# The carry of a chunked scan added by identity matmuls, a contraction over pairs of time steps, and stores issued from ScalarE

## The reference

```
deltaBC = layernorm(x) @ W_bc.T          # gives dt_r (64), B (32), C (32) of each time step
delta   = softplus(dt_r @ W_dt.T + b_dt)                    # (b, l, d)
for t in time:
    h = exp(delta_t * A) * h + (delta_t * u_t) * B_t        # (b, d, n), fp32
    y_t = sum over n of h * C_t                             # (b, d)
x = x + y + u * D_param                                     # then the second layer
```

## Time and profile before

| | us |
|---|---|
| median of 3 runs | 1120.57 |
| the profiled execution | 1123.69 |
| its span, first to last instruction | 1122.0 |
| VectorE busy | 964.6 (86%) |
| TensorE busy (matmuls) | 911.9 (81%) |
| TensorE weight loads | 562.7 (50%) |
| ScalarE busy | 460.1 (41%) |
| GpSimd busy | 392.1 (35%) |

### The profile page before, as it was taken

One profiled execution on the slowest core, in us unless ns is written; L12 is line 12 of the kernel. 1 busy time (PEld: TensorE's weight loads), 2 busy tenths in 40 slices (PEclk: granted clock), 3 DMA queues, 4 the chain that ended last, 5 costly groups with the idle time before them and its releaser, 6 DMA issues. The chain is left out here.

```text
span 1122.0 us, 22454 instructions
## 1 busy us (share of the span) xinstructions
PE 911.9 (81%) x7152; PEld 562.7 (50%) x7152; DVE 964.6 (86%) x1164; ACT 460.1 (41%) x887; POOL 392.1 (35%) x690
## 2 busy tenths in 40 slices
PE   5654673489999999999999999999997856666662
PEld 4343442356656656556566566565553444343442
DVE  6664664099999999999999999999998599999993
ACT  2545544434444444444444444444431333333320
POOL 6435432233333333333333333333343244444321
PEclk9675555589999999999999999999998977787786
DMA  9399995931211112121111211111142001111001
GB/s 319 64 147 205 162 135 131 134 108 50 64 52 59 54 52 64 51 62 53 59 55 50 66 51 61 55 55 57 52 139 70 16 0 57 56 56 56 19 19 37
DMA packets 206068, 85.68 MB, mean 76 GB/s; under 512 B 139220, under 2 KB 196052, under 8 KB 205268
## 3 DMA queue, kind: packets, MB, share of 16 engines
q1 hardware_dynamic: 206036, 85.30, 31.9%
HBM read 45.85 MB, written 39.42 MB: 76 GB/s over the span
## 5 line engine op out<-in xcount | busy, mean ns | idle before, releaser
L1439 DVE TENSOR_TENSOR_SCAN arena<-arena,psum 128x1024 f32<-128x1024 f32 x256 | 585.4, 2287 | 8.9
L1260 ACT ACTIVATE arena<-psum 128x512 f32<-128x512 f32 x512 | 281.9, 605 | 347.5 <-PE psum L1123 346.1
L1167 PEld LDWEIGHTS psum<-du_mov,b_sta 96*128 96x128 bf16 x2048 | 199.7, 130 | 237.2 <-issue 217.3
L1136 PE MATMUL psum<-arena,c_sta 128*32 128x256 f32 x2048 | 284.0, 636 | 2.7 <-DVE arena L1439 2.7
L1167 PE MATMUL psum<-du_mov,b_sta 96*128 96x128 bf16 x2048 | 271.2, 313 | 15.2 <-DVE arena L1439 15.2
L1018 POOL TENSOR_TENSOR carry<-arena 128x64 f32<-128x64 f32 x252 | 117.0, 464 | 399.2 <-DVE arena L1439 390.5
L1123 PE MATMUL psum<-delta_mov,a_sta 96*128 96x128 bf16 x2048 | 171.6, 228 | 8.3 <-ACT arena L1260 8.3
L1123 PEld LDWEIGHTS psum<-delta_mov,a_sta 96*128 96x128 bf16 x2048 | 151.9, 110 | 11.3 <-ACT arena L1260 10.2
L1021 POOL TENSOR_TENSOR arena<-zeros 128x64 f32<-128x64 f32 x256 | 78.1, 305 | 20.1
L1436 DVE TENSOR_TENSOR psum<-psum,carry 128x64 f32<-128x64 f32 x256 | 55.3, 216 | 31.3 <-DMA delta_terms<-arena 30.8
L433 PE MATMUL psum<-delta_mov,arena 128*128 128x512 f32 x128 | 75.7, 677 | 0.0
(11 more groups left out here) (142 smaller groups left out, 962.8 us busy)
## 6 DMA issues: line engine op xcount, KB each, us to landing
du_terms<-arena SPq DMA_DIRECT2D x48, 256.0 KB, 3.8
du_mov<-du_terms SPq DMA_DIRECT2D x128, 96.0 KB
b_terms<-delta_mov SPq DMA_DIRECT2D x6, 1024.0 KB, 11.3
delta_terms<-arena SPq DMA_DIRECT2D x48, 128.0 KB, 5.3
delta_mov<-delta_terms SPq DMA_DIRECT2D x128, 48.0 KB
b_sta<-b_terms SPq DMA_DIRECT2D x64, 96.0 KB
arena<-in_L_attn_x SPq DMA_DIRECT2D x8, 512.0 KB, 5.5
base<-arena SPq DMA_DIRECT2D x8, 512.0 KB, 4.7
```

What stands on the lines that cost most here:

```text
L1136: mm = nc.tensor.matmul(psum[32 * j:32 * j + 32, (6 + k) * BANK:(6 + k) * BANK + D], c_sta[k][:, t * 32:(t + 1) * 32], sub(arena, 0, P, (2 ...
L1167: mm = nc.tensor.matmul(sub(psum, 0, P, o, (4, 4), (TS, GD // 2)), b_sta[k][0:ROWS, (s * 4 + tg) * P:(s * 4 + tg + 1) * P], sub(du_mov[k], ...
L1260: nc.scalar.activation(sub(arena, 0, P, k * CHUNK_ELEMS + u * 16 * TS, (TS, 16), (D * TS, SUBS), (1, TS)), sub(psum, 0, P, (4 + u % 2) * B ...
L1439: nc.vector.tensor_tensor_scan(state[s][:, seg], decay[k][:, (s * D + g * GD) * TS:(s * D + (g + 1) * GD) * TS], psum[:, 2 * (step % 2) * ...
```

## The change

Three parts, and what goes with them.

1. The carry is added on TensorE. After each filling, TensorE waits for the carry and runs two fp32 matmuls (one for each bank of the pair) with the 128x128 identity as weights and 32 columns of the carry moving, accumulated onto the first time step of every channel. VectorE's add and its semaphore `carried` go. In a filling the order is now by half first, and the stationary of the first four time steps comes last. GpSimd waits for `b_ready` in place of `carried` before it makes a carry again.
2. The contraction takes two neighbouring time steps per matmul: 512 columns (256 channels x 2), weights for both steps side by side (16 of the 32 columns each), so half of the output is not used. There are half as many matmuls, issued in groups 0 and 2 only, and `contract_done` comes at group 2. GpSimd writes the weights with two instructions, and ScalarE takes y out with two copies, each of every other column.
3. y is stored from ScalarE's queue, behind the exponentials of step 6, with eight DMAs of 16 rows of 1 KB in place of four of 32 rows from SyncE.

```diff
+TP = 2
+SETS = TS // (4 * TP)
+Y_STORES = 4 * TP
...
@@ SyncE
-            def store_y(c, k):
-                settle(sp_)
-                sp_.wait_ge(S["y_evac"], c + 1)
-                for j in range(4):
-                    sp_.dma_start(dram(y_d, c * (TC * D) + j * D, (4 * D, TC // 4), (L * D, B), (1, D)),
-                                  y_rows[k][32 * j:32 * j + 32, :]).then_inc(y_stored[k], 16)
...
@@ GpSimd
-                    pool.tensor_tensor(
-                        sub(c_sta[k], 0, P, 0, (4 * 32 + 4, TC // 4), (32, 4), (1, B)),
...
+                    for u in range(TP):
+                        pool.tensor_tensor(
+                            sub(c_sta[k], 0, P, u * 4 * B, (4 * 32 + B, 4), (32, 4), (1, B)),
...
                             if not early:
+                                pool.wait_ge(S["b_ready"], G - 3)
                                 pool.wait_ge(S["scan_done"], G - 3)
-                                pool.wait_ge(S["carried"], G - 3)
...
@@ TensorE
-            def contract(c, k, s, quads):
-
-                for qq in quads:
+            def contract(k, s, sets):
+
+                for r in sets:
                     for j in range(4):
-                        t = s * TS + 4 * qq + j
-                        q = t // 4
+                        pi = SETS * s + r
                         mm = nc.tensor.matmul(
-                            psum[32 * j:32 * j + 32, (6 + k) * BANK:(6 + k) * BANK + D],
-                            c_sta[k][:, t * 32:(t + 1) * 32],
-                            sub(arena, 0, P, (2 * CHUNK_ELEMS + s * D * TS) + 4 * qq + j, (TS, D)),
-                            start=(q == 0), stop=(q == TC // 4 - 1), skip_group_check=True)
+                            psum[32 * j:32 * j + 32, (6 + k) * BANK:(6 + k) * BANK + TP * D],
+                            c_sta[k][:, (pi * 4 + j) * 32:(pi * 4 + j + 1) * 32],
+                            sub(arena, 0, P, (2 * CHUNK_ELEMS + s * D * TS) + TP * (4 * r + j), (TS, D), (1, TP)),
+                            start=(pi == 0), stop=(pi == SETS * SUBS - 1), skip_group_check=True)
...
-                            for tg in range(TS // 4):
-                                for half in range(2):
+                            for half in range(2):
+                                for tg in (1, 2, 3, 0):
...
+                            pe.wait_ge(S["carry_ready"], G + 1)
+                            for half in range(2):
+                                mm = nc.tensor.matmul(
+                                    sub(psum, 0, P, (pair_bank + half) * BANK, (TS, GD // 2)), ident[:, :],
+                                    carry[:, g, half * (GD // 2):(half + 1) * (GD // 2)],
+                                    start=False, stop=True, skip_group_check=True)
                             mm.then_inc(S["b_ready"], 1)
...
-                                mm = contract(pc, pk, ps, [g])
-                                if g == 3:
+                                if g % 2 == 0:
+                                    mm = contract(pk, ps, [g // 2])
+                                if g == 2:
                                     mm.then_inc(S["contract_done"], 1)
...
@@ ScalarE
+            def y_copies(k):
+
+                for u in range(TP):
+                    nc.scalar.copy(y_rows[k][:, u * D:(u + 1) * D], sub(psum, 0, P, (6 + k) * BANK + u, (TP, D)))\
+                        .then_inc(S["y_evac"], 1)
+
+            def y_stores(c, k):
+
+                act.wait_ge(S["y_evac"], TP * (c + 1))
+                for u in range(TP):
+                    for j in range(4):
+                        p0 = 32 * j + 16 * u
+                        act.dma_start(dram(y_d, c * (TC * D) + (TP * j + u) * D, (4 * TP * D, 4), (L * D, B), (1, D)),
+                                      y_rows[k][p0:p0 + 16, u * D:(u + 1) * D]).then_inc(y_stored[k], 16)
...
+                            y_copies(1 - k)
+                        if step == 6 and not (first and k == 0):
+                            y_stores(c - 1, 1 - k)
...
+            y_copies(1)
+            y_stores(CHUNKS - 1, 1)
             phase_f_act(act)
@@ VectorE
-                            firsts = sub(psum, 0, P, 2 * (step % 2) * BANK, (TS, GD))
-                            nc.vector.tensor_tensor(firsts, firsts, carry[:, g, :], ALU.add)\
-                                .then_inc(S["carried"], 1)
-                            dve.wait_ge(S["carried"], G + 1)
```

More of the change, by code:

```diff
@@ L109, in build @@
         carry = sb("carry", [P, 4, GD])
-        y_rows = [sb(f"y_rows{k}", [P, D]) for k in range(2)]
+        y_rows = [sb(f"y_rows{k}", [P, 2 * D]) for k in range(2)]
         ident = sb("ident", [P, P])
@@ L443, in start @@
                 transposes(1, 1)
-                pe.wait_ge(S["y_evac"], CHUNKS)
+                pe.wait_ge(S["y_evac"], TP * CHUNKS)
             def gate_transposes(lt, seen):
@@ L908, in m_pair @@
                         f_load(sp_, 1, 1)
-                    if not (first and k == 0):
-                        store_y(c - 1, 1 - k)
                     if not last:
@@ L916, in _ @@
             tiles(sp_, CHUNKS // 2, m_pair)
-            store_y(CHUNKS - 1, 1)
             phase_f_sync(sp_)
@@ L1191, in _ @@
             pe.wait_ge(S["scan_done"], CHUNKS * STEPS)
-            contract(CHUNKS - 1, 1, 1, range(4)).then_inc(S["contract_done"], 1)
+            contract(1, 1, range(SETS)).then_inc(S["contract_done"], 1)
             phase_f_pe(pe)
@@ L1286, in m_pair @@
                             if not (isinstance(n, int) and n <= 0):
-                                act.wait_ge(y_stored[1 - k], 64 * n)
-                            nc.scalar.copy(y_rows[1 - k][:, :],
-                                           bank(7 - k)[:, 0:D])\
-                                .then_inc(S["y_evac"], 1)
+                                act.wait_ge(y_stored[1 - k], 16 * Y_STORES * n)
+                            y_copies(1 - k)
+                        if step == 6 and not (first and k == 0):
+                            y_stores(c - 1, 1 - k)
             m_pair(0, True, False)
@@ L1299, in _ @@
             act.wait_ge(S["contract_done"], 2 * CHUNKS)
-            act.wait_ge(y_stored[1], 64 * (CHUNKS // 2 - 1))
-            nc.scalar.copy(y_rows[1][:, :], bank(7)[:, 0:D]).then_inc(S["y_evac"], 1)
+            act.wait_ge(y_stored[1], 16 * Y_STORES * (CHUNKS // 2 - 1))
+            y_copies(1)
+            y_stores(CHUNKS - 1, 1)
             phase_f_act(act)
```

18 lines of the change are left out of this document (9 added, 9 removed).

## The result

The changed kernel takes 1308.86 us (median of 4 runs, 1295.99 to 1312.13) against 1120.57 before: a ratio of 1.165, with a 95% interval of 1.159 to 1.172. It is slower, as forecast, but by 188 us where the forecast had 96, and above the top of its range. The profiled execution took 1308.35 us, with a span of 1306.6.

A forecast was written before the change was run, and what follows sets the result against it. TensorE was taken to set the pace, with VectorE about 0.1 us per chunk behind. The sum was 1123.69 - 6 + 98 + 4.6 = 1220.3, so about 1217 us for the median run, range 1090 to 1250.

The forecast's parts named there:

- Identity and pairs, without stall: TensorE in the scan phase: a chunk takes 19.56 us against 19.75, over 31 chunks -6 us.
- Stall by the issues, full clock: TensorE waits for step 7's exponentials behind eight ScalarE issues: 3.55 us a chunk in the loop, 1.95 outside, +98 us.
- Lower clock after the stall: TensorE's clock falling after each stall: nothing in the sum, some 25 us at the top of the range.
- The end: The last eight stores, 5.5 us, stand ahead of ScalarE's first work of the next phase: +4.6 us.
- What bounds the kernel: Scan phase: TensorE sets the pace, VectorE is about 0.1 us per chunk behind; work taken from VectorE alone gains almost nothing.
- rival C: Contraction: pairs read no faster, wave 0.91 us; 1231 us with hidden issues, near 1310 with the stall; chance 0.08.
- handoff waits: Every fourth step's contraction on TensorE waits for the scan before it: 0.36 us, twice a chunk.
- rivals A and B: ScalarE's issues hide: A about 1118 us, chance 0.12; B, identity weights also load behind fillings, about 1083, chance 0.20.
- deciding point, 0.44 per issue: ScalarE's queue: eight issues end before TensorE's need if one costs at most 0.44 us.
- 50 ns of dispatch: Cost of starting a DMA by the skill's table; by that the stores would be hidden and the sum -6 us.
- rival D: TensorE's clock falls after stalls: up to 1.7 us per chunk, some 25 us, about 1250; top of the forecast's range.

The follow-up runs named there:

- experiment 1: Changed kernel with its eight stores still on ScalarE, but one behind each step's exponentials instead of all in step 6: 1111.45 us, ratio 0.991.
- experiment 2: Changed kernel with 14 unused bf16 matmuls of 512 columns ahead of step 0's arguments, where the gap is: 1196.89 us, ratio 1.067.
- experiment 5: Kernel before plus identity alone, 1214.40 us; that plus eight stores on ScalarE in step 6, 1313.08; changed kernel with add back on VectorE, no identity, 1244.89.
- experiment 7: Changed kernel with its eight stores issued from SyncE again, identity and pairs kept: 1136.18 us, ratio 1.013.
- (9): Experiment 1's kernel without identity matmuls, add back on VectorE: 1151.16 us; with contractions moved to groups 1 and 3, 1120.25.

## Why the prediction was right or wrong, by its steps

| Term | Forecast | Measured | From |
|---|---|---|---|
| Identity and pairs, without stall | -6 | -18.0 | experiment 1 against before, first to last scan |
| Stall by the issues, full clock | +98 | +90.9 | experiment 2 against 1, the same stretch |
| Lower clock after the stall | 0; at most about 25 | +106.7 | changed kernel against experiment 2 |
| The end | +4.6 | +4.9 | behind the last scan |
| Sum | +96.6 | +184.5 | the span grew by 184.6 |

**What bounds the kernel: right.** TensorE's pace; without VectorE's add nothing is won (5), and every microsecond on TensorE is nearly paid in full.

**Identity and pairs: right in their prices, the sum small by 12 us.** An identity is 0.41 where 0.45 stood, a pair contraction 1.05 where 1.06 did, so the earlier trace rows had been the right row to choose: a wave of 512 columns in pairs costs what 256 single ones did, and rival C is refuted. Arguments ahead of a filling are 0.45, not 0.49. Eight times 0.04 and four times 0.04 are 0.5 us of a chunk, some 15 us in 31 chunks. The handoff waits were right in kind, 0.43 in the mean for 0.36. In all a chunk is 19.04 and not 19.56. The first chunk went the other way, from 19.57 to 22.78, for a reason that no run looks into. One reading was off without effect: from first to second wave (1.12 - 0.64) is 0.48, not 0.46; the earlier trace rows give 0.45.

**The stall: mechanism, place and count right.** An issue on ScalarE takes 0.64 (0.66 to 0.79 had been read on SyncE for the larger stores), 0.79 from one to the next in the loop (0.92), so eight take 6.18 and not 7.1. The gap is 3.03 and not 3.55. There are 29, as forecast. The issues could not hide: rivals A and B fell at their own deciding point, 0.44 per issue. The Trainium skill ("DMA: Bandwidth & Descriptors", Issuing engines are not separate DMA queues) takes the time to start a DMA as usually small beside the DMA itself; 6.18 us per chunk in ScalarE's order speak against counting it as nothing here, and experiment 1 shows when it costs nothing: one at a time, each in an idle time of its own. The 50 ns of dispatch that the prediction took from that page of the Trainium skill stand there for DMAs issued from GpSimd, which these are not.

**The failing step is rival D's price.** "A spell as long as each stall, 3.5 us of work at half the rate ... where half of the chunks have it, that is some 25 us", and of this the sum held nothing. Both halves were wrong. The spell isn't as long as the gap, it is some 10 us for a gap of 3 (500.88 to 511.60), and one follows every gap but the first (28 in the scan phase by the clock's records, 6.8 to 13.7 us each, 283 in all). That costs 3.86 us per chunk, more than the stall itself. The words also mix two sums: a spell of 3.5 us at half the rate loses 1.7, but 3.5 us of work at half the rate lose 3.5. The earlier trace rows had shown that the clock falls when TensorE is idle; what I took from them was the length of the idle time, when what counts is how much work is done before the clock is back, and the trace of before had no such place in the loop. Outside it there was one, and I read it only for the price of a wave: in the earlier trace rows TensorE is busy for 3.30 of 3.30 us and the clock is 0.50 all the same. The bound from above for such a cost is the work up to the next gap at half the rate, about 19 us more per chunk (an estimate, the 19.04 of experiment 1 done in twice the time), not a gap's length; with that end kept, the range would have held the result.
The Trainium skill ("TensorE: Matmul & The Clock Gate", Loop structure matters more than you think) says that a loop in which every matmul stands behind a long wait runs them at the lower clock and one in which they follow on each other does not; experiment 2 agrees, with 1.00 against the changed kernel's 0.80, although here there is one gap in a chunk and not one before each matmul.

**The end: right**, 4.9 for 4.6.

**What stays open.** Why a spell lasts 10 us at all, with TensorE busy, and why it does so with identity and pairs together while with either alone, or with neither, nearly all spells are 3.4 or 6.8 us. The gap's length alone does not decide it (experiment 5). Nor is it settled why the pairs without the identity (9) fell to the lower clock without a gap for ScalarE.

## What to carry to other kernels

A DMA on a compute engine's queue is an instruction of that engine, in its order: count issues times pitch against the time until someone needs the next result behind them, and spread them, one in each idle time, rather than in a block (eight in one block 1309 us, four and four 1110). A new gap on TensorE of even 1.5 to 3 us in a loop is to be priced twice, once as idle time and once as work at 1.2 GHz after it, which can be more than the gap. Where a gap can't be removed, test whether idle matmuls in it pay; here they gave back 112 us.

## What the runs showed that I had not expected

- After a gap of 3.09 us TensorE's granted clock stood at 0.56 in the mean for the next 10.2 us, with TensorE busy for 10.11 of them. Being busy by the profile did not bring the clock back at once.
- Pairs make the contraction depend on the clock: 1.87 against 1.05 us, where single columns took 1.12 at the lower level. At the full clock one contraction of pairs (1.05) replaces two of single columns (2.12), at 1.2 GHz 1.87 replaces 2.24: most of the gain is gone.
- Fourteen useless matmuls per chunk made the kernel 9% faster (1196.89 against 1308.86).
- The issues of the new, smaller stores follow each other a little faster on ScalarE than on SyncE: 0.79 from one to the next, against 0.85 there ((6.62 - 0.64) / 7). One by itself takes 0.64 on either (median 637 ns on SyncE in experiment 7, 633 on ScalarE in the changed kernel). The old stores on SyncE took 0.92.
- With the contractions in the groups that have no scan just before them, the chunk fell from 19.04 to 18.27 although no work was removed: the handoff wait, 0.36 us in the prediction and a small correction there, was worth 24.0 us from first to last scan, more than the 18.0 that the change gained at full clock.
